# A fused graph network on one core: the engines' loops over pairs of batches written out, VectorE's waiting memsets removed

## What is computed

```
x = _layernorm(x + _L0_gnn_ref(x, adj, ...))    # attention, one head
x = _layernorm(x + _L1_gnn_ref(x, adj, ...))    # 3 blocks: attention + FFN 256->1024->256
x = _layernorm(x + _L2_gnn_ref(x, adj, ...))    # attention that keeps the 16 largest weights
x = _layernorm(x + _L3_gnn_ref(x, adj, ...))    # 8 heads of 32 features
```

## Time and profile before

| | |
|---|---|
| time, median of 3 runs | 3546.47 us (3540.43 to 3549.6) |
| the profiled execution's own time | 3541.92 us |
| its span, first to last instruction | 3540.0 us |
| instructions in the trace | 58799 |
| busy share of the span | PE 93%, PEld 73%, DVE 70%, ACT 60%, POOL 21% |
| mean granted TensorE clock | 0.961 of full speed |

### The profile page before, as it was taken

The page is one execution under the profiler, slowest core; times in us unless marked ns, Lnnn a source line. Parts: engine busy times, 40 slices in busy tenths (PEclk is TensorE's granted clock), DMA queues, the critical chain, the costliest instruction groups (busy, mean ns, idle before and its releaser), DMA issues.

```text
span 3540.0 us, 58799 instructions
## 1 busy us (share of the span) xinstructions
PE 3281.3 (93%) x18240; PEld 2578.6 (73%) x18240; DVE 2468.1 (70%) x7925; ACT 2135.9 (60%) x4289; POOL 740.2 (21%) x1052
## 2 busy tenths in 40 slices
PE   6699999999999999999999999999999999999976
PEld 5587777877777687777877778677777777778664
DVE  3567786767767767677767867767786667867655
ACT  3356566665665756656665666756657665666634
POOL 1221221222221221221222221222221222221210
PEclk8899999999999999999999999999999999999989
DMA  5000000000000000000000000000000000000000
GB/s 147 1 1 13 7 13 8 7 7 7 13 8 9 6 7 13 8 13 7 7 7 8 13 7 7 7 8 13 7 13 7 2 13 7 13 7 1 1 7 7
DMA packets 39843, 40.11 MB, mean 11 GB/s; under 512 B 7264, under 2 KB 38240, under 8 KB 39520
## 3 DMA queue, kind: packets, MB, share of 16 engines
q1 hardware_dynamic: 31072, 27.68, 2.6%
q0 software_dynamic: 8448, 8.39, 1.6%
HBM read 36.07 MB, written 8.39 MB: 13 GB/s over the span
## 4 chain that ended last, share of the span: by engine, by line
PE 41%; issue 41%; POOL 9%; DVE 7%; ACT 1%; POOLq 0%; DMA 0%; DVEq 0%; SPq 0%; ACTq 0%
PE work L1260 8%; PE acc L1274 7%; PE acc L1236 5%; POOL rstd L512 4%; PE acc L1340 4%; PE acc L1309 3%; PE acc L1321 3%; PE work L1321 3%; POOL R L520 2%; POOL R L524 2%; PE work L1289 2%; DVE HX L803 2%; PE work L1177 1%; PE work L1221 1%; DVE T L690 1%
## 5 line engine op out<-in xcount | busy, mean ns | idle before, releaser
L512 POOL TENSOR_TENSOR rstd<-var_eps,minus_half 128x2 f32<-128x2 f32 x320 | 226.3, 707 | 2702.7 <-DVE var_eps L798 2702.7
L1260 PE MATMUL work<-XT,w_sb 128*128 128x256 f32 x3072 | 729.1, 384 | 17.2 <-ACT XT L1042 7.0
L1274 PE MATMUL acc<-w_sb,gT 128*128 128x256 f32 x3072 | 735.4, 386 | 0.0
L1274 PEld LDWEIGHTS acc<-w_sb,gT 128*128 128x128 f32 x3072 | 581.0, 193 | 110.0 <-issue 34.1
L1260 PEld LDWEIGHTS work<-XT,w_sb 128*128 128x128 f32 x3072 | 557.2, 190 | 140.5 <-ACT gT L1052 29.5
L1052 ACT ACTIVATE gT<-work,b_sb 128x256 f32<-128x256 f32 x768 | 347.6, 472 | 244.5 <-PE work L1260 241.4
L1236 PE MATMUL acc<-X,PT 128*128 128x256 f32 x1536 | 355.7, 385 | 0.9 <-ACT PT L1020 0.7
L1236 PEld LDWEIGHTS acc<-X,PT 128*128 128x128 f32 x1536 | 286.0, 191 | 69.8 <-issue 14.1
L998 ACT ACTIVATE PT<-T,s 128x512 f32<-128x512 f32 x192 | 124.4, 711 | 246.7 <-DVE T L707 245.4
L789 DVE BATCH_NORM_STATS2 stats<-R 128x6 f32<-128x256 f32 x640 | 240.9, 418 | 11.0
L1236 PE MATMUL acc<-V,PT 128*128 128x256 f32 x1024 | 234.7, 382 | 3.7 <-ACT PT L1020 3.7
(11 more groups left out here) (160 smaller groups left out, 5877.2 us busy)
## 6 DMA issues: line engine op xcount, KB each, us to landing
HX<-in_x SPq DMA_DIRECT2D x16, 512.0 KB, 3.8
pos<-in_adj POOLq DMA_DIRECT2D x16, 512.0 KB, 5.5
out<-X SPq DMA_DIRECT2D x32, 256.0 KB, 2.1
w_sb<-in_L_gnn_W SPq DMA_DIRECT2D x6, 1024.0 KB, 8.2
g_sb<-in_L_gnn_g SPq DMA_DIRECT2D x6, 128.0 KB, 6.6
awr_sb<-in_L_gnn_attn_w SPq DMA_DIRECT2D x2, 256.0 KB, 7.6
c_sb<-in_L_gnn_beta SPq DMA_DIRECT2D x3, 128.0 KB, 4.3
PT<-in_L_gnn_b SPq DMA_DIRECT2D x3, 128.0 KB, 5.8
```

Of the source, the lines that this page charges most:

```text
L512: pool.tensor_tensor(rstd[s][:, half_rows(half)], var_eps[s][:, half_rows(half)], minus_half[:], ALU.pow)\
L1260: last = pe.matmul(u.bank[:, 0:HN], w1_sb[:, l, c, f * P:(f + 1) * P], XT[s][:, c, half * HN:(half + 1) * HN], start=(c == 0), stop=(c == ...
L1274: last = pe.matmul(acc[s][half][:, i, :], gT[s][:, f, i * P:(i + 1) * P], w2_sb[:, l, f, :], start=(f == 0 and i == 0), stop=(f == FC - 1) ...
```

## The change

`with engine.Fori(0, PAIRS - 1) as it:` becomes `for it in range(PAIRS - 1):` on all five engines. The program is then straight code from end to end, each wait is for a number, and there is no branch and no register instruction left in it. `mark()` and all its calls go, so that each custom pass, `bn_aggr`, `max` and `match_replace` carries its wait. The order of the work, the tiles, the arithmetic and the transfers stay.

```diff
-        marked = sb("marked", [P, 32], BF16)
...
-            with sp.Fori(0, PAIRS - 1) as it:
+            for it in range(PAIRS - 1):
                 walk(it, to_a, stages)
                 walk(it + 1, to_b, stages)
...
-            with pool.Fori(0, PAIRS - 1) as it:
+            for it in range(PAIRS - 1):
...
-            places = itertools.cycle(range(32))
-
-            def mark():
-
-                at = next(places)
-                dve.memset(marked[:, at:at + 1], 0.0)
-
...
                     for t in tiles(half):
                         dve.wait_ge(rectified.sems[s], rectified.value(it, key, t))
-                        mark()
                         there = (T[s][:, t, :], T[s][:, t, :], PT[s][:, t, :])
...
                 dve.wait_ge(stats_ready.sems[s], stats_ready.value(it, key, half))
-                mark()
                 for t in tiles(half):
                     last = dve.bn_aggr(mean_var[s][:, t, :], stats[s][:, t, :])
...
-            with dve.Fori(0, PAIRS - 1) as it:
+            for it in range(PAIRS - 1):
...
-            with act.Fori(0, PAIRS - 1) as it:
+            for it in range(PAIRS - 1):
...
-            with pe.Fori(0, PAIRS - 1) as it:
+            for it in range(PAIRS - 1):
```

More of the change, by code:

```diff
@@ L1 @@
 from contextlib import ExitStack
-import itertools
 import concourse.bass as bass
```

## The result

| | before | after |
|---|---|---|
| median of 4 runs each, us | 3543.45 (3537.99 to 3549.6) | 3501.89 (3500.36 to 3504.46) |
| the profiled execution / its span | 3541.92 / 3540.0 | 3500.57 / 3498.8 |
| instructions in the trace | 58799 | 51849 |
| time outside PE's busy time | 258.7 | 255.1 |

The ratio is 0.9884, interval [0.9867, 0.9901]: the changed kernel is 1.2% faster, by 41.6 us, where 17 were forecast.

The account below looks back on a forecast made before the run. PE was taken as the bound, with only its 259 us of standing time to win. Branches 10.0, registers 3.5 and memsets 3.8 summed to 17.3 us, from 3546.5 to 3529 us, range 3511 to 3541.

Parts of the forecast that it names:

- What bounds the kernel: PE, busy 3281.3 of 3540.0 us; without taking matmuls away, edits can win only the 259 us in which it stands.
- The branches: PE's gaps at L1177, six taken branches 9.2 us plus loop entry 0.8: 10.0 us gained, bounds 8 and 10.5.
- The waits on registers: VectorE's register instructions before L855, ahead of PE's L1148 transposes: 3.5 us gained, bounds nothing and about 3.8.
- The memsets: 1088 on VectorE, 0.02 us each where VectorE is last: 3.8 us gained, bounds 1.2 and 15.
- The sum: Branches 10.0, registers 3.5 and memsets 3.8 make 17.3 us; 3546.5 less this gives 3529 us.
- Rival 1: Shorter waits let clock steps fall out: 14 us more, 3515 us; 3504 with memsets at full length; chance 0.13.
- Rival 2: Most gain lost again through clock phase, other engines' branches and a moved L855 stall: 5.5 us left, 3541 us; chance 0.15.
- Rival 3: Straight code stalls PE at each of 170 fetched instruction blocks: slower, 3614 us at 0.5 us each; chance 0.07.

Follow-up runs that it names:

- e9: Kernel before with all five loops, registers and memsets kept, and a prefetch hint for each loop's closing branch: 3534.93 us, ratio [0.9967, 0.9996].
- e4: Kernel before with only PE's loop written out, memsets kept: 3543.72 us, ratio [0.9980, 0.9999].
- e2: Kernel before with all loops kept and each memset replaced by a VectorE semaphore increment that carries the wait: 3590.19 us, ratio [1.0100, 1.0145].
- e14: Kernel before with all loops but VectorE's written out, VectorE's branch prefetched, memsets kept: 3521.92 us, ratio to before [0.9938, 0.9971].
- e1: Kernel before with all five loops written out and the 1088 memsets kept: 3500.04 us, ratio [0.9843, 0.9876].
- e16: Changed kernel with six scratch memsets ahead of L838's sum, once a pass: 3499.05 us, ratio to before [0.9872, 0.9905].
- e17: Changed kernel with fifteen scratch memsets ahead of L838's sum, once a pass: 3524.92 us, ratio to before [0.9926, 0.9959].
- e18: Changed kernel with one bn_stats of 128x128 ahead of L838's sum, once a pass: 3523.25 us, ratio to before [0.9923, 0.9956].
- e11: Kernel before with all loops but VectorE's written out, memsets kept: 3542.70 us, ratio [0.9991, 1.0016].

## Why the prediction failed, step by step

- **What bounds the kernel.** The step that failed is its first: "all that any edit here can win without taking matmuls away is the 259 us in which PE stands". PE stood 255.1 us after, so that account changed by 3.6 us and PE's busy time by 37.6. The prediction's check, PE's busy time "within 5 us of before", is wrong by the same 37.6 us. The closing pass, in which nothing but memsets changed, gained 5.6 us in this way.
- **The branches**, 10.0 us forecast. e9 removes them alone and measures 9.4 us of standing time and 7.5 us of time, inside the bounds of 8 and 10.5 by the first and just below them by the second. The size was right for all engines' branches together. The text speaks of PE's; e4 shows that PE's alone is worth nothing that can be told, since ACT's and VectorE's stalls stand behind it. Of the 0.64 us at the loop's entry, 0.40 are there in straight code too, so the jump's part of the 0.8 us was 0.2.
- **The waits on registers**, 3.5 us forecast. As standing time the number was right: PE's L1148 wait fell by 3.7 us over the span. The cause was right in part: registers have 0.10 us in each of the 14 passes, 1.4 us, and 0.35 us in seven passes, 2.5 us, were the stall that is also gone with registers kept (e2, e9). The prediction had this doubt ("the 0.37 us can be a place where VectorE's instruction stream crosses from one fetched block to the next"), and its sign for it, 0.3 us more at that wait in some passes, came in one pass. As time the term was far too small: e14 against e1 puts 22 us on VectorE's register instructions, nearly all of it PE's busy time.
- **The memsets**, 3.8 us forecast, measured nothing that can be told (e1). The aggregation pair of the earlier trace rows takes 0.25 us with its memset (2141.63 to 2141.88), and 0.25 in after without one. The high bound took a memset at its full 59 ns. e16 and e17 contradict that: six in the chain ahead of PE's wait cost it 0.04 us together, and fifteen in a row take 0.24 us, 0.016 each. The Trainium skill's some 60 ns for each VectorE operation ("Perfetto Trace Analysis", section on optimizing Scalar/DVE operations) agrees with a memset's length in the profile, but not with what one adds in a row.
- **The sum.** Branches and registers gave 12 us of standing time, and other waits took back about 8: the heads' group, and the wait at L1203, 16 times instead of 11. The sum held nothing for either sign of this. Standing and clock hang together, too: in e18's passes the third of the heads' waits is 0.72 us where the lower level holds for 6.8 us just there and 1.18 where it holds for 3.4, so a PE that works faster stands more.
- **Rival 1** is what happened, and it was sized at 14 us and given 0.13. Its case was that a step of the clock can fall out when waits get shorter; what spoke against it was that "the gaps shrink by a tenth to a third of a microsecond and stay where they are". e18 shows that two tenths are enough, and e14 that one may be. A step at half of the passes, 2 us each, was too small: there are 77 us less at the lower level in 15 passes, 2.6 us of PE's time in each. Its far end, 3504 us, is near the result by luck: 11 of its 25 us below the forecast are the memsets' full length, and they are worth nothing that can be told.
- **Rival 2** has the right mechanism too, in that the phase of the clock decides more than the gaps; its sign was wrong here. **Rival 3**, a stall at each fetched block, did not come: in after PE has three "issue" waits of 0.5 us or less, 1.4 us together, of which before had two with 1.0, and the blocks fell by 20 and 49 on the two queues. Its smaller form is there: VectorE has four such waits of 0.3 us, and the one at L838, in the eighth pass, goes with three drops.

**What stays open:** which of the three places drops in a given pass, and so why all loops written out end at 99 to 106 us of lower clock and each subset at 143 or more. The runs show that it depends on delays of 0.1 to 0.2 us; the passes alternate in patterns that hold for many passes; no rule was found that gives the number ahead of a run.

## What to carry to other kernels

When PE is busy for nearly all of a repeating pass, as here (199 to 203 of 209 to 212 us), and its granted clock is below 1, compare several passes of the same work first. If PE's busy time differs between them, a change of a tenth or two of a microsecond in one wait can be worth many times its own size (21 us for 2.7 in e18), in either direction, and the range has to hold that. Stalls of several engines at one place (here their branches) must be removed together, and a prefetch hint on the branches takes them away without writing the program out. Test a theory about such a gain by putting a small delay back in one place, not only by undoing the edit.

## What the runs showed of the hardware that was not expected

- A delay of 0.18 us in one wait per pass made TensorE's busy time 20.8 us longer with the same matmuls (e18 against after), and 0.04 us made no difference (e16).
- 1088 semaphore increments that carry waits on VectorE, ahead of custom passes and aggregations, made PE stand 27.6 us longer, and the aggregation shown starts 0.11 us later (e2); memsets in their place cost nothing that can be told (e1).
- The taken branches stall VectorE for 2.3 to 2.5 us (e11), ScalarE for 2.2 to 2.5 (e4) and TensorE for 1.2 to 1.6 (before); with the hint on the back edge none of these shows (e9, e14).
- A stall of 0.35 us on VectorE, ended by "issue", moves with the program's layout: it stands in seven passes of before, in none of e2, and in one of after.
- VectorE's scaling of two tiles beside GpSimd's issue of a transfer takes 2.36 us with GpSimd's loop and 1.65 without; what in it is held, and by what, was not tried.
